# Decoder layer on one core: tokens laid four consecutive to a partition, and the context scan split into row sums and one triangular product

## The reference

```python
def _L0_xattn_ref(q, k, v):
    DECAY = 0.9
    kv = jnp.swapaxes(k * v, 0, 1)

    def step(r, kv_t):
        r = DECAY * r + kv_t
        return (r, r)
    r0 = jnp.zeros(q.shape[:1] + q.shape[2:], dtype=q.dtype)
    _, rs = jax.lax.scan(step, r0, kv)
    return q * jnp.swapaxes(rs, 0, 1)

x = _layernorm(x + _L0_attn_ref(x, ...), axis=-1)
x = _layernorm(x + _L0_xattn_ref(x, ctx_1024, ctx_1024), axis=-1)
x = _layernorm(x + _L0_ffn_ref(x, ...), axis=-1)
```

## Time and profile before

| | |
|---|---|
| median of three runs | 2942.02 us (2941.82 to 2942.49) |
| the profiled execution, its own time | 2942.34 us |
| its span, first to last instruction | 2940.6 us |
| mean granted TensorE clock | 0.965 of 2.4 GHz |
| TensorE matmul busy | 2698.1 us, 92% of the span |
| VectorE busy | 2122.7 us, 72% |
| ScalarE busy | 1264.8 us, 43% |
| GpSimd busy | 513.3 us, 17% |
| context load `csq<-in_ctx_rows` | 16 x 1024 KB, 6.1 us from issue to landing |

### The profile page before, as it was taken

One profiled execution on the slowest core, in us unless ns is written; L12 is line 12 of the kernel. 1 busy time (PEld: TensorE's weight loads), 2 busy tenths in 40 slices (PEclk: granted clock), 3 DMA queues, 4 the chain that ended last, 5 costly groups with the idle time before them and its releaser, 6 DMA issues.

```text
span 2940.6 us, 33446 instructions
## 1 busy us (share of the span) xinstructions
PE 2698.1 (92%) x12016; PEld 2217.1 (75%) x12016; DVE 2122.7 (72%) x2561; ACT 1264.8 (43%) x1426; POOL 513.3 (17%) x305
## 2 busy tenths in 40 slices
PE   2489999999999999849999998899999969999998
PEld 2477777777777777638888887688888858888886
DVE  8668888888888888834444445587788776666664
ACT  2234333344343444333333332788888842222222
POOL 4211111111111111200000000122222223234332
PEclk7789999999999999979999999899999989999999
DMA  6311111211111111144545443677767673555453
GB/s 233 117 43 58 58 57 58 74 61 57 57 57 57 62 66 58 58 168 154 171 157 162 154 155 133 239 268 260 259 250 259 252 272 125 207 233 210 185 209 126
DMA packets 146957, 429.21 MB, mean 146 GB/s; under 512 B 74848, under 2 KB 83296, under 8 KB 106592
## 3 DMA queue, kind: packets, MB, share of 16 engines
q1 hardware_dynamic: 143312, 402.43, 37.7%
q10 hardware_dynamic: 3600, 26.22, 2.2%
HBM read 234.62 MB, written 177.21 MB: 140 GB/s over the span
## 4 chain that ended last, share of the span: by engine, by line
PE 52%; DVE 2%; DMA 1%; issue 1%; ACT 1%; POOL 0%; SPq 0%; POOLq 0%; DVEq 0%
PE ff_ps L1652 12%; PE ff_ps L1653 12%; PE ff_ps L1654 12%; PE ff_ps L1689 5%; PE ff_ps L1690 5%; PE ff_ps L1691 5%; DMA ff_w_stage<-w_ffn_t 1%; DVE ff_wl L1368 0%; DVE ff_sr L1574 0%; DMA ff_cand_g<-gate_ints 0%; DVE ff_lo L1374 0%; DVE ff_up_abs L1406 0%; DMA ff_q<-x_ints 0%; DMA gate_products<-ff_group 0%; ACT ff_wh L1202 0%
## 5 line engine op out<-in xcount | busy, mean ns | idle before, releaser
L1652 PE MATMUL ff_ps<-ff_hi,ff_wh 128*128 128x512 f32 x1536 | 600.0, 391 | 63.1 <-DVE ff_lo L1374 63.1
L1653 PE MATMUL ff_ps<-ff_lo,ff_wh 128*128 128x512 f32 x1536 | 599.5, 390 | 0.0
L1654 PE MATMUL ff_ps<-ff_hi,ff_wl 128*128 128x512 f32 x1536 | 599.4, 390 | 0.0
L1219 ACT ACTIVATE ff_group<-ff_ps,ff_scales 128x512 f32<-128x512 f32 x384 | 259.1, 687 | 333.7 <-PE ff_ps L1654 320.0
L1652 PEld LDWEIGHTS ff_ps<-ff_hi,ff_wh 128*128 128x128 f32 x1536 | 289.6, 189 | 124.2 <-DVE ff_lo L1374 63.9
L1654 PEld LDWEIGHTS ff_ps<-ff_hi,ff_wl 128*128 128x128 f32 x1536 | 289.5, 188 | 60.5
L1653 PEld LDWEIGHTS ff_ps<-ff_lo,ff_wh 128*128 128x128 f32 x1536 | 289.6, 189 | 60.3
L1689 PE MATMUL ff_ps<-ff_wh,ff_hi 128*128 128x512 f32 x768 | 300.1, 391 | 25.7 <-DVE ff_lo L1590 24.7
L1690 PE MATMUL ff_ps<-ff_wl,ff_hi 128*128 128x512 f32 x768 | 299.7, 390 | 0.0
L1691 PE MATMUL ff_ps<-ff_wh,ff_lo 128*128 128x512 f32 x768 | 299.7, 390 | 0.0
L1385 DVE TENSOR_REDUCE ff_gate_max<-ff_group 128x2048 f32 (+1 forms) x48 | 109.7, 2286 | 221.9 <-ACT ff_group L1219 221.9
(11 more groups left out here) (197 smaller groups left out, 5341.9 us busy)
## 6 DMA issues: line engine op xcount, KB each, us to landing
gate_products<-ff_group SPq DMA_DIRECT2D x48, 1024.0 KB, 4.0
ff_raw<-gate_products SPq DMA_DIRECT2D x48, 1024.0 KB, 5.6
up_products<-ff_group SPq DMA_DIRECT2D x48, 1024.0 KB, 4.2
ff_raw<-up_products SPq DMA_DIRECT2D x48, 1024.0 KB, 9.2
gate_ints<-ff_gs SPq DMA_DIRECT2D x48, 512.0 KB, 2.6
ff_gs<-gate_ints SPq DMA_DIRECT2D x48, 512.0 KB, 9.9
xt_raw<-in_xT SPq DMA_DIRECT2D x64, 256.0 KB, 2.8
csq<-in_ctx_rows SPq DMA_DIRECT2D x16, 1024.0 KB, 6.1
```

The costliest lines, as they stand in the source:

```text
L1219: act.activation(group[:, g, m * T:(m + 1) * T], out_ps[(GM * g + m) % 6][:], ACT.Copy, scale=s_x).then_inc(evacuated, 1)
L1652: pe.matmul(o, wh[:, m, k], hi[:, par, k], start=(k == 0), stop=False)
L1653: pe.matmul(o, wh[:, m, k], lo[:, par, k], start=False, stop=False)
L1654: mm = pe.matmul(o, wl[:, m, k], hi[:, par, k], start=False, stop=(k == KC - 1))
```

## The change

Tokens now lie as t = 4 p + j: a partition holds four consecutive tokens. The recurrence splits into three parts. Within a partition, three row sums on VectorE add 0.9 times the row before (`local_sums`, `csq[:, j] += 0.9 csq[:, j-1]`). Over partitions, the last row's sums are multiplied by one strictly triangular 128x128 matrix of powers of 0.9^4 on TensorE, three matmuls instead of 30 (`context_carry`). Then VectorE adds 0.9^(j+1) times the carried sum to each of the four rows (`carried_sums`). The second residual reads `csq` in SBUF instead of a PSUM bank.

ScalarE squares the context instead of GpSimd, and makes the high half of one row instead of four; VectorE makes the low half of that row (`last_sum_low`), instead of GpSimd of all four. GpSimd keeps the roots alone. The product stands between `qkv(s, 2)` and `qkv(s, 3)` on TensorE instead of at the step's end, and in the last step ahead of the projection. Projection tile j loads every fourth column of `ah` and `al` as weights, a step of 16 bytes, and tile 1 waits for the carried sums. The context's load waits until the second residual has read `csq`. The host passes the rows without a transpose, and the output rows need none.

```diff
@@ -267,8 +267,8 @@
-        csq_h = sb("csq_h", [P, TT, HID], F32R)
-        csq_l = sb("csq_l", [P, TT, HID], F32R)
+        csq_h = sb("csq_h", [P, HID], F32R)
+        csq_l = sb("csq_l", [P, HID], F32R)
@@ -312,7 +312,7 @@
-        scan_banks = [mix_ps[0][:], mix_ps[1][:], qk_ps[1][:, 0], qk_ps[1][:, 1]]
+        carry_bank = mix_ps[0][:]
@@ -354,7 +355,7 @@
-                        wait(sp, sql_ready, s)
+                        wait(sp, y_ready[1], TT * s)
                         sp.dma_start(csq[:], ctx_in[s]).then_inc(ctx_landed, 16)
@@ -414,11 +415,6 @@
                 def step(s, front, back):
                     if back:
-
-                        pool.wait_ge(ctx_landed, 16 * s)
-                        pool.tensor_tensor(csq[:], csq[:], csq[:], ALU.mult).then_inc(sq_ready, 1)
-                        pool.wait_ge(sqh_ready, s)
-                        pool.tensor_tensor(csq_l[:], csq[:], csq_h[:].bitcast(F32), ALU.subtract).then_inc(sql_ready, 1)
                         root(0, s)
                         root(1, s)
@@ -472,12 +468,14 @@
                             act.activation(ah[:, m], att[:, m], ACT.Copy).then_inc(mh_ready, 1)
+                        act.wait_ge(ctx_landed, 16 * s)
+                        act.activation(csq[:], csq[:], ACT.Square).then_inc(sq_ready, 1)
                     if front:
                         front_tile(s, 1, par)
                     if back:
-                        act.wait_ge(sq_ready, s)
-                        wait(act, scan_ready, TT * (s - 1) if not isinstance(s, int) or s > 1 else 0)
-                        act.activation(csq_h[:], csq[:], ACT.Copy).then_inc(sqh_ready, 1)
+                        act.wait_ge(summed, (TT - 1) * s)
+                        wait(act, carry_ready, s - 1)
+                        act.activation(csq_h[:], csq[:, TT - 1], ACT.Copy).then_inc(sqh_ready, 1)
@@ -565,13 +563,32 @@
+                def local_sums(s):
+
+                    dve.wait_ge(sq_ready, s)
+                    for j in range(1, TT):
+                        dve.scalar_tensor_tensor(csq[:, j], csq[:, j - 1], XDECAY, csq[:, j],
+                                                 ALU.mult, ALU.add).then_inc(summed, 1)
+                        dve.wait_ge(summed, (TT - 1) * (s - 1) + j)
+
+                def last_sum_low(s):
+                    dve.wait_ge(sqh_ready, s)
+                    dve.tensor_tensor(csq_l[:], csq[:, TT - 1], csq_h[:].bitcast(F32), ALU.subtract).then_inc(sql_ready, 1)
+
+                def carried_sums(s):
+
+                    dve.wait_ge(carry_ready, s)
+                    for j in range(TT):
+                        dve.scalar_tensor_tensor(csq[:, j], carry_bank, XDECAY ** (j + 1), csq[:, j],
+                                                 ALU.mult, ALU.add).then_inc(scanned, 1)
+
                 def second_residual(s, tiles):
...
-                        dve.wait_ge(scan_ready, n)
-
-                        dve.scalar_tensor_tensor(xrow[:, j], scan_banks[j], 1.0, xrow[:, j],
+                        dve.wait_ge(scanned, n)
+
+                        dve.scalar_tensor_tensor(xrow[:, j], csq[:, j], 1.0, xrow[:, j],
                                                  ALU.add, ALU.mult).then_inc(y_ready[1], 1)
@@ -649,9 +666,21 @@
                     if front:
                         front_product(s, 0)
-                        for c in range(1, KC):
-                            front_scans(s, c, par)
-                            front_product(s, c)
+                    if back:
+                        local_sums(s)
+                    if front:
+                        front_scans(s, 1, par)
+                        front_product(s, 1)
+                    if back:
+                        last_sum_low(s)
+                    if front:
+                        front_scans(s, 2, par)
+                        front_product(s, 2)
+                    if back:
+                        carried_sums(s)
+                    if front:
+                        front_scans(s, 3, par)
+                        front_product(s, 3)
@@ -753,11 +782,13 @@
-                        if j < 2:
-                            pe.wait_ge(gated, KC * (s - 1) + j + 3)
+                        if j == 0:
+                            pe.wait_ge(gated, KC * (s - 1) + 3)
+                        elif j == 1:
+                            pe.wait_ge(scanned, TT * s)
                         else:
                             pe.wait_ge(y_ready[0], TT * (s - 1) + j - 1)
-                        stat = [(ah[:, k, j * P:(j + 1) * P], al[:, k, j * P:(j + 1) * P]) for k in range(KC)]
+                        stat = [tuple(h[:, k].rearrange("p (q j) -> p j q", j=TT)[:, j] for h in (ah, al)) for k in range(KC)]
@@ -783,17 +814,10 @@
-                def context_scan(s, front):
+                def context_carry(s):
                     pe.wait_ge(sql_ready, s)
-                    for j in range(TT):
...
-                        product(scan_banks[j], stat, mov).then_inc(scan_ready, 1)
+                    pe.wait_ge(gated, KC * s)
+                    product(carry_bank, [(strip_h[:], strip_l[:])], [(csq_h[:], csq_l[:])]).then_inc(carry_ready, 1)
@@ -803,6 +827,10 @@
                         for c in range(1, KC):
                             qkv(s, c)
+                            if back and c == 2:
+                                context_carry(s)
+                    elif back:
+                        context_carry(s)
@@ -821,8 +849,6 @@
                     if front:
                         broadcast(s)
-                    if back:
-                        context_scan(s, front)
```

More of the change, by code:

```diff
@@ L284, in attention_phase @@
         head_bc = sb("head_bc", [2 * NH, KC, P], F32R)
-        stripf = kv[:, 0]
+        stripf = kv[:, 0, 0:P]
         bc_high = qks[0:2 * NH, 0].rearrange("p (c m) -> p c m", m=P)
         bc_low = qks[0:2 * NH, 1].rearrange("p (c m) -> p c m", m=P)
-        strip_h = sb("strip_h", [P, T], F32R)
-        strip_l = sb("strip_l", [P, T], F32R)
+        strip_h = sb("strip_h", [P, P], F32R)
+        strip_l = sb("strip_l", [P, P], F32R)
         head_sum = sb("head_sum", [P, KC, NH])
@@ L339, in attention_phase @@
         norm_ready = [sem("norm1_ready"), sem("norm2_ready")]
-        sq_ready, sqh_ready, sql_ready, scan_ready = sem("sq_ready"), sem("sqh_ready"), sem("sql_ready"), sem("scan_ready")
+        sq_ready, sqh_ready, sql_ready, carry_ready = sem("sq_ready"), sem("sqh_ready"), sem("sql_ready"), sem("carry_ready")
+        summed, scanned = sem("summed"), sem("scanned")
         amax_step_ready, amax_taken = sem("amax_step_ready"), sem("amax_taken")
@@ L386, in _ @@
                 pool.memset(mhalf[:], -0.5).then_inc(const_pool, 1)
-                pool.memset(c09[:], XDECAY).then_inc(const_pool, 1)
+                pool.memset(c09[:], XDECAY ** TT).then_inc(const_pool, 1)
                 pool.memset(amax_x2[:], 0.0).then_inc(const_pool, 1)
@@ L398, in _ @@
                 pool.affine_select(out=stripf, in_=stripf, compare_op=ALU.not_equal, fill=1.0,
-                                   base=0, pattern=[[-1, T]], channel_multiplier=1).then_inc(const_pool, 1)
+                                   base=1, pattern=[[-1, P]], channel_multiplier=1).then_inc(const_pool, 1)
                 for rows, base in ((bc_high, 0), (bc_low, NH * D)):
@@ L517, in _ @@
                 dve.wait_ge(const_pool, NPOOL)
-                dve.tensor_tensor_scan(stripf, c09[:, 0:1].to_broadcast([P, T]), stripf, 0.0,
+                dve.tensor_tensor_scan(stripf, c09[:, 0:1].to_broadcast([P, P]), stripf, 0.0,
                                        ALU.mult, ALU.add).then_inc(const_dve, 1)
@@ L784, in broadcast @@
                         pe.matmul(bc_banks[c], head_bc[:, c], rec_turned[:], start=True, stop=True).then_inc(bc_ready, 1)
-                def context_scan(s, front):
+                def context_carry(s):
                     pe.wait_ge(sql_ready, s)
-                    for j in range(TT):
-                        if j < 2:
-                            pe.wait_ge(y_ready[0], TT * s - j)
-                        elif front:
-                            pe.wait_ge(o_ready, KC * s + j - 1)
-                        stat = [(strip_h[:, (j - i) * P:(j - i + 1) * P], strip_l[:, (j - i) * P:(j - i + 1) * P])
-                                for i in range(j + 1)]
-                        mov = [(csq_h[:, i], csq_l[:, i]) for i in range(j + 1)]
-                        product(scan_banks[j], stat, mov).then_inc(scan_ready, 1)
+                    pe.wait_ge(gated, KC * s)
+                    product(carry_bank, [(strip_h[:], strip_l[:])], [(csq_h[:], csq_l[:])]).then_inc(carry_ready, 1)
                 def step(s, front, back):
@@ L1729 @@
         "xT": np.ascontiguousarray(a["x"].transpose(0, 2, 1)).reshape(NB, KC, P, T),
-        "x_rows": np.ascontiguousarray(a["x"].reshape(NB, TT, P, HID).transpose(0, 2, 1, 3)),
```

(5 more changed lines are left out.)

## The result

The changed kernel takes 2953.8 us, the median of seven runs (2952.71 to 2955.17); the kernel before, on the same chip, 2942.97 (2941.82 to 2944.73, seven runs). The ratio is 1.0037, with a 95% interval from 1.0026 to 1.0047: slower by 10.8 us, beyond what a measurement can mistake for no change. The forecast said no change. The time lies in its range.

What follows compares the result with a forecast made beforehand. TensorE's nearly closed chain bounds the attention phase, with gate stalls and a wait for VectorE at the step's end. Terms -10.4 + 30.8 - 37.0 + 10.2 + 4.3 = -2.1 us from 2942.34 give 2940.2 us; range 2924 to 2965.

Steps and rivals of the forecast that it cites:

- the projection's weights: Projection's weight loads at a step of 16 bytes: taken as nothing; lower end nothing, upper end +154 us.
- Starts over 0.23 us apart in the projection: Projection matmuls starting this far apart: named as a sign that the forecast was wrong.
- Rival 2: Projection's strided weight loads bind TensorE: mild end +0.02 each, +15, 2955 us; at three times, 3011 us; chance 0.20.
- The scan matmuls: Step's end: 30 matmuls go, but qkv still waits for VectorE's xl; gains 0.74 us at 14 boundaries, -10.4 us.
- The clock: TensorE's 6.1 us idle before each qkv(s, 0) halves the clock; slow restart costs 2.2 us, 14 times, +30.8 us.
- Rival 1: At the step boundary the clock doesn't fall, or the gap closes: 2909.4 us; if it falls half the times, 2925; chance 0.10.
- GpSimd's hold: Gate: GpSimd's big operations slow VectorE's scans and stall TensorE twice; moving them gains 2.64 us in 14 steps, -37.0 us.
- The product: Triangular product: three matmuls in TensorE's full stretch, 0.68 us each of 15 times, +10.2 us.
- Rival 3: The product waits: 0.1 us slack, VectorE's chain 1 us later stalls qkv(s, 3) and projection; +14 us, 2954 us; chance 0.12.
- The last step: Product ahead of the projection with no front half to cover it; 18.0 us where 13.7 were needed, +4.3 us.
- that row's 0.50 us: Matmul at 1222.64, behind 4.15 us idle, recorded with 0.50 us: read as the clock not yet fallen, for the clock-doesn't-fall case.

Runs made afterwards that it cites:

- The experiment by token tile: Changed kernel with low halves 2 and 3 of the next x earlier, plus mix halves read at 16-byte step and written packed, so projection weights are packed: 2936.81 us.
- 4 scan matmuls: Kernel before with the context's square on ScalarE, and only 4 of the 30 context scan matmuls kept, one per output tile: 2925.53 us.

## Why the prediction was right and wrong

**The step that failed** is the projection's weights: "I take nothing, since even twice the time stays under the matmul it hides behind". The strided load is recorded with 315 ns where the packed one has 191, and the projection takes 0.78 us more a step, 0.016 a matmul on average. The average hides that most of it stands at five places a step, four of them in tile 1, behind the denominators' short matmuls. Weight loads and matmuls there, first in the kernel before, then in the changed kernel:

```profile
713.17 0.19 PEld L721 LDWEIGHTS mix_ps<-wah,al 128*128 128x128 f32 x1
713.28 0.19 PEld L717 LDWEIGHTS mix_ps<-wah,ah 128*128 128x128 f32 x1
...
713.20 0.48 PE L721 MATMUL mix_ps<-wah,al 128*128 128x512 f32 x1
713.52 0.39 PE L717 MATMUL mix_ps<-wah,ah 128*128 128x512 f32 x1
```

```profile
785.98 0.31 PEld L750 LDWEIGHTS mix_ps<-wah,al 128*128 128x128 f32 x1
786.20 0.33 PEld L746 LDWEIGHTS mix_ps<-wah,ah 128*128 128x128 f32 x1
...
786.01 0.60 PE L750 MATMUL mix_ps<-wah,al 128*128 128x512 f32 x1
786.45 0.40 PE L746 MATMUL mix_ps<-wah,ah 128*128 128x512 f32 x1
```

Two loads that follow each other without a long matmul between them start 0.11 us apart when packed, as the prediction worked out (107 ns), and 0.22 apart at the step: twice, which is what the prediction allowed. But here no 512-column matmul covers the first of them, and the next matmul comes after 0.44 us instead of 0.32. The fifth place is behind the turned reciprocals, ahead of tile 3. On average over 13 steps these five intervals went from 0.31 to 0.44 us, +0.63 a step; the 37 intervals between covered loads went only from 0.228 to 0.235, +0.26; the rest of the projection gave back 0.11. With packed weights in the changed kernel the five are at 0.31 again, and with strided ones in the kernel before at 0.43. So "the matmul it hides behind" is what failed: most of the cost comes from the few loads that hide behind none. Why the covered ones also stand at 0.235, a little over 0.227, is not shown. Starts over 0.23 us apart in the projection were one of the signs that the prediction named.

Rival 2's mild end had +0.02 a matmul, +15 us, 2955 us, with a chance of 0.20; the runs say 12.7 us in the kernel before and 15.0 in the changed one. It had the amount and not the place: it too took every load as covered. Where a row is missing and the sum is near zero, the sign hangs on that term.

The Trainium skill (SBUF — State Buffer, "Specifications (TRN2)") states that each crossing into a new 16-byte line pays a penalty. The trace agrees: 191 ns became 315. ScalarE's copy went from 625 to 1116 ns and VectorE's subtraction from 683 to 1074 in the one experiment where these read at that step.

**The scan matmuls**: forecast -0.74 a boundary, measured -0.64. The mechanism held: TensorE idle 6.2 us (forecast 6.1), released by `xl`.

**The clock**: forecast 2.2 us a boundary from three restarts, measured 1.75 and 2.75 in turn, 2.25 on average. Rival 1 is out. The term is shown by two opposite experiments: filling the stretch gave back 26.5 us, and opening it in a kernel without the rest of the change cost 21.2 although 5.9 us of work a step were gone.

**GpSimd's hold**: forecast -2.64 us a step and -37 in all. The gate measures 10.88, and the square's move alone gives 38.4 us. Why a GpSimd instruction of 3.60 us holds VectorE's scan is not shown; that the scan is held beside it and not without it, is.

**The product**: forecast 0.68, measured 0.71 and 0.80 in turn. Rival 3's thin slack held: `csq_l` ends at 772.70 and the product starts at 772.84, at full pitch. One step later 0.06 us are left (842.22 to 842.28), and the product takes 0.80. The experiment by token tile lengthened that chain and the wait came.

**The last step**: forecast +4.3 us, measured +5.3.

The sum with the measured terms is -0.64 + 2.25 - 2.64 + 0.75 + 0.78 = +0.50 us a step, 7.0 in 14, and 5.3 at the end: 12.3 us. The profiled executions differ by 12.8 in their spans (that of the changed kernel is the slowest of its seven), the medians by 10.8. Without the strided loads, 16 x 0.77 = 12.3, it would have been 0: the rest of the forecast's sum, -2.1, was right to about 2 us, single terms to 1.4.

What stays open: why the restart's loss alternates from step to step (1.75, 2.75). It is no fixed price: with packed weights it went 2.9, 2.1, 1.8, 1.6, 1.4 over five steps and then began at 3.0 again, and with 4 scan matmuls, in steps of 68.3 us, it settled at 2.1.

## What to carry to other kernels

Work that fills another engine's wait is free, and removing it can cost more than it takes: ask what TensorE does in the hole, and count the restart, here 1.4 to 3.0 us each and about 2.2 on average. A change with several parts should be priced apart: the move of one instruction, worth 38.4 us by itself, paid for most of a rewrite whose other parts cost about 49. A cost taken as hidden, without a row and near the limit of its cover, deserves its own measurement before the sum is trusted, and a look at what covers each instance of it: five uncovered loads a step made most of this one.

## What the runs showed that was not expected

- The clock does not have to fall at once. Behind a gap of 2.47 us six matmuls ran at full pitch and then eight at the low one. The kernel before has it too: at 1222.64, behind 4.15 us, the first interval is 0.34 and the second 0.23, and from 1223.21 on they are 0.43. The prediction took that row's 0.50 us as a clock that had not fallen; it fell two matmuls later, and windows show it: a granted clock of 0.99 from 1222.7 to 1223.2 us and of 0.50 from 1223.3 to 1226.5:

```profile
1222.98 0.44 PE L718 MATMUL mix_ps<-al,wah 128*128 128x512 f32 x1
1223.21 0.63 PE L721 MATMUL mix_ps<-ah,wal 128*128 128x512 f32 x1
1223.64 0.63 PE L717 MATMUL mix_ps<-ah,wah 128*128 128x512 f32 x1
```

- So it is not enough to read the first matmul behind a gap; the starts of the next fifteen tell. Gaps of 0.56 and of 1.42 to 1.48 us showed no fall, gaps of 2.47 and 3.40 did.
- A step of 16 bytes cost each of three engines: a weight load 1.65 times, a ScalarE copy 1.8 times, a VectorE subtraction 1.6 times.
- Removing a loss that another engine's order already covers gave nothing, even though it was plain in the trace: 2924.0 us with a clock at half in part of every step, 2925.06 without.
